# Decoder layer on one core: ten of sixteen states taken through both channel halves together, five scale operations, new tables of places

## What is computed

```python
def step(state, inp):
    d, b, c, u = inp
    dA = jnp.exp(d[..., None] * A)
    state = state * dA + (d * u)[..., None] * b[:, None, :]
    y = jnp.einsum('bdn,bn->bd', state, c)
    return (state, y)
```

```python
gamma_x = jnp.clip(jnp.max(jnp.abs(x), axis=-1, keepdims=True), 1e-05, None)
scale_x = 127.0 / gamma_x
x_dq = jnp.clip(jnp.round(x * scale_x), -128.0, 127.0) / scale_x
gamma_w = jnp.clip(jnp.mean(jnp.abs(w)), 1e-05, None)
w_dq = jnp.clip(jnp.round(w / gamma_w), -1.0, 1.0) * gamma_w
```

## Time and profile before

| | us |
|---|---|
| median of 3 runs | 993.59 |
| lowest and highest | 993.3, 995.66 |
| the profiled execution | 995.87 |
| span of its trace | 994.1 |
| PE busy | 818.1 |
| DVE busy | 797.5 |
| ACT busy | 591.6 |
| POOL busy | 479.0 |
| mean granted TensorE clock | 0.907 of full |

### The profile page before, as it was taken

How to read it: one execution, slowest core, us unless ns; L and a number is a source line. 1 busy time by engine, 2 the same in 40 slices (tenths; PEclk the granted TensorE clock), 3 DMA queues, 4 the chain that set the end, 5 groups by cost and what they waited for, 6 DMA issues and landing times.

```text
span 994.1 us, 11740 instructions
## 1 busy us (share of the span) xinstructions
PE 818.1 (82%) x4066; PEld 452.4 (46%) x4066; DVE 797.5 (80%) x953; ACT 591.6 (60%) x865; POOL 479.0 (48%) x283
## 2 busy tenths in 40 slices
PE   5778787465888889898877889896988799997798
PEld 1425445232553335564452434564564345663344
DVE  5869876696898988888897976978688997956874
ACT  3779779984277864633466766443366876443443
POOL 0546975684536625464437443365406664562010
PEclk9778997768799999998988999988999899999699
DMA  8677688767516636667436454575605675763000
GB/s 296 240 207 216 177 257 230 220 170 202 126 34 152 134 76 159 161 137 168 101 74 152 110 119 98 123 173 134 139 1 127 145 159 137 168 147 72 0 12 32
DMA packets 54815, 138.79 MB, mean 140 GB/s; under 512 B 7683, under 2 KB 8067, under 8 KB 54757
## 3 DMA queue, kind: packets, MB, share of 16 engines
q0 software_dynamic: 16128, 58.73, 31.1%
q1 hardware_dynamic: 38628, 79.32, 25.1%
HBM read 74.96 MB, written 4.35 MB: 80 GB/s over the span
## 4 chain that ended last, share of the span: by engine, by line
PE 42%; DVE 35%; ACT 14%; issue 7%; DMA 1%; DVEq 0%; POOL 0%; SPq 0%; ACTq 0%; POOLq 0%
PE bank L754 16%; DVE W L1738 11%; PE bank L967 7%; DVE PB L1727 6%; PE bank L783 4%; DVE U L1696 3%; PE bank L984 3%; ACT DEC L1203 3%; PE bank L802 3%; DVE BST L1673 2%; PE bank L861 2%; ACT W L1326 2%; PE bank L839 2%; DVE ARENA L1771 1%; DVE HAM L1891 1%
## 5 line engine op out<-in xcount | busy, mean ns | idle before, releaser
L1580 POOL TENSOR_TENSOR W<-W,CROW 128x1024 f32<-128x1024 f32 x128 | 321.1, 2509 | 239.2 <-DVE W L1738 188.1
L1738 DVE TENSOR_TENSOR_SCAN W<-DEC,PB 128x1024 f32<-128x1024 f32 x125 | 285.7, 2286 | 14.3 <-ACT DEC L1203 6.1
L1593 POOL DMA_DIRECT2D ACC<-W x112 | 98.4, 879 | 166.2 <-DMA ACC<-W 147.8
L1727 DVE TENSOR_TENSOR PB<-DU,PB 128x1024 f32<-128x1024 f32 x128 | 156.5, 1223 | 25.5 <-PE PB L923 21.2
L1203 ACT ACTIVATE DEC<-DT,ACOL 128x511 f32<-128x511 f32 x250 | 160.1, 710 | 21.4 <-DVE W L1738 20.3
L967 PE MATMUL bank<-W,ARENA 128*128 128x512 fp8e4 x512 | 127.8, 395 | 0.0
L923 PE MATMUL PB<-BC,ID 96*128 96x512 bf16 x128 | 50.7, 421 | 60.8 <-DVE W L1738 58.8
L1163 ACT ACTIVATE ARENA<-bank 128x512 f32<-128x512 f32 x56 | 32.3, 590 | 92.0 <-PE bank L754 51.0
L967 PEld LDWEIGHTS bank<-W,ARENA 128*128 128x128 bf16 x512 | 46.1, 100 | 66.2 <-issue 23.7
L1883 DVE SCALAR_TENSOR_TENSOR ARENA<-bank,SDQ,ARENA 128x512 f32<-128x512 f32 x64 | 46.8, 740 | 33.3 <-ACT ARENA L1303 15.3
L1303 ACT ACTIVATE ARENA<-bank,SDQ 128x512 f32<-128x512 f32 x64 | 43.1, 685 | 49.7 <-PE bank L967 49.4
(11 more groups left out here) (172 smaller groups left out, 1349.6 us busy)
## 6 DMA issues: line engine op xcount, KB each, us to landing
ACC<-W POOLq DMA_DIRECT2D x112, 512.0 KB, 4.8
CROW<-c_rows SPq DMA_DIRECT2D x128, 256.0 KB, 3.6
W<-in_wffn SPq DMA_DIRECT2D x27, 512.0 KB, 7.0
X<-in_wffn SPq DMA_DIRECT2D x21, 512.0 KB, 5.9
X<-in_x SPq DMA_DIRECT2D x7, 1024.0 KB, 8.2
out_dram<-X SPq DMA_DIRECT2D x16, 256.0 KB, 2.2
X<-in_ctxT SPq DMA_DIRECT2D x4, 512.0 KB, 4.7
ARENA<-in_x SPq DMA_DIRECT2D x1, 1024.0 KB, 6.4
```

The lines of the kernel that those rows point to most:

```text
L1580: pool.tensor_tensor(w, w, CROW[u % 2][:, :].unsqueeze(1).broadcast_to([P, 2, L]), ALU.mult)\
L1593: pool.dma_start(ACC[accumulator(u)][:, :, :], w, accum_op=ALU.add).then_inc(y_summed, 16)
L1727: dve.tensor_tensor(into, du, rows, ALU.mult).then_inc(dbu_done.sem, 1)
L1738: dve.tensor_tensor_scan(flat(W[u % 4]), flat(decay_of(u)), flat(PB[:, u % 2:u % 2 + 2, :]), 0.0, ALU.mult, ALU.add).then_inc(scan_done.se ...
```

## The change

**Order of the units.** In rows 2 to 4 states 0 to 5 of half 0 come first, then states 6 to 15 with half 0 and half 1 in turn, then states 0 to 5 of half 1. A unit with the same state as the one before it is `joined`: it has no spread and no row of C of its own. SPREAD_OF numbers the spreads, and their banks and the buffers CROW go by that number. The first unit of a pair keeps the spread's bank and writes the two others (`scan_bank`), so the next spread waits for that unit's scan (`spread_freed`).

**Step sizes of blocks 2 and 3.** On PE they move behind point r2, on ACT behind the gate's SiLU; in the list of products behind `wo`. DU for these blocks is made after unit 3. The skip term of half 1 moves from after r6 to after r5, ahead of the norm's `rstd`.

**Scales.** The division by 127 goes into the clipping, the reciprocal gives the scale directly, and the scales of both weights are made by one product each: five operations for eight.

**Tables.** All counts are set anew; the absolute sums, the ternary steps and the two reductions of row 1 have tables too (STEP_SUMS, STEP_TERNS, STEP_GAMMA), and a chunk's ternary step now stands one or two chunks behind its scaling.

```diff
+        out += on(four, [(b, "dt", 2), (b, "dt", 3)])
...
-        out += on(four, [(b, "dt", 2), (b, "dt", 3)])
...
-    [(('r', 0), 1), (('r', 1), 1), (('r', 2), 1), (('r', 3), 0), (('r', 4), 0), (('r', 5), 0), (('r', 6), 0),
-     (('r', 7), 2), (('r', 8), 4), (('f', 0, 0), 0), (('f', 0, 1), 0), (('f', 0, 2), 0), (('f', 0, 3), 2),
+    [(('r', 0), 2), (('r', 1), 1), (('r', 2), 1), (('r', 3), 0), (('r', 4), 1), (('r', 5), 1), (('r', 6), 0),
+     (('r', 7), 1), (('r', 8), 3), (('f', 0, 0), 0), (('f', 0, 1), 1), (('f', 0, 2), 1), (('f', 0, 3), 0),
...
-DU_AFTER = (28, 12)
+DU_AFTER = (28, 3)
...
+ALONE = 6
+HALVES_FIRST = [(h, n) for h in range(2) for n in range(N)]
+STATES_FIRST = ([(0, n) for n in range(ALONE)] + [(h, n) for n in range(ALONE, N) for h in range(2)]
+                + [(1, n) for n in range(ALONE)])
...
-    return b, j // N, j % N
+    return (b, *(STATES_FIRST if b else HALVES_FIRST)[j])
+def joined(u):
+    return u > 0 and unit(u)[::2] == unit(u - 1)[::2]
+def spread_freed(k):
+    return FIRST_WITH[k - 1] if FIRST_WITH[k - 1] < LAST_WITH[k - 1] else LAST_WITH[k - 2]
+def scan_bank(u):
+    upper = SPREAD_OF[u] % 2
+    return upper if u == LAST_WITH[SPREAD_OF[u]] else 1 - upper
...
@@ c_row (SP) @@
+                if joined(u):
+                    return
+                k = SPREAD_OF[u]
-                if u >= 2:
-                    sp.wait_ge(*hc_done.at(0, u - 1))
+                if k >= 2:
+                    sp.wait_ge(*hc_done.at(0, LAST_WITH[k - 2] + 1))
...
@@ spread_b, units (PE) @@
-                if u >= 2:
-                    pe.wait_ge(*scan_done.at(0, u - 1))
+                k = SPREAD_OF[u]
+                if k >= 2:
+                    pe.wait_ge(*scan_done.at(0, spread_freed(k) + 1))
...
-                    spread_b(u)
+                    if not joined(u):
+                        spread_b(u)
...
@@ step (PE) @@
                     units(b, "r", 2)
+                    step_size(b, 2)
+                    step_size(b, 3)
...
                 units(b, "r", 8)
-                if new:
-                    step_size(b, 2)
-                    step_size(b, 3)
...
@@ step (ACT) @@
                     gate_z(f, t)
+                if new:
+                    act.preload_act_table_set("softplus")
+                    step_size(b, 2)
+                    step_size(b, 3)
                 exp_and_log()
...
                 decays(b, "r", 5)
+                if new:
+                    skip_term(b, 1)
                 rstd(f, 2)
...
-                if new:
-                    skip_term(b, 1)
...
                     decays(b, "q")
-                    act.preload_act_table_set("softplus")
-                    step_size(b, 2)
-                    step_size(b, 3)
                     act.preload_act_table_set("silu_and_others")
...
@@ inputs_b, scan (DVE) @@
-                rows = PB[:, 2 * (u % 2), :].unsqueeze(1).broadcast_to([P, 2, L])
-                if u % 2:
+                rows = PB[:, 2 * (SPREAD_OF[u] % 2), :].unsqueeze(1).broadcast_to([P, 2, L])
+                if scan_bank(u):
...
@@ row_scales (DVE) @@
-                dve.tensor_scalar(AMC[:, :], AMX[:, :], 1e-5, None, ALU.max).then_inc(q_step.sem, 1)
+                dve.tensor_scalar(AMC[:, :], AMX[:, :], 1e-5, 1.0 / 127, ALU.max, ALU.mult).then_inc(q_step.sem, 1)
                 dve.wait_ge(*q_step.at(f, 2))
-                dve.reciprocal(RIN[:, :], AMC[:, :]).then_inc(q_step.sem, 1)
+                dve.reciprocal(SXQ[:, :], AMC[:, :]).then_inc(q_step.sem, 1)
+                dve.tensor_tensor(SDQ[:, :, :], AMC[:, :].unsqueeze(1).broadcast_to([P, 2, TT]),
+                                  GAM[:, 0:2].unsqueeze(2).broadcast_to([P, 2, TT]), ALU.mult).then_inc(q_step.sem, 1)
                 dve.wait_ge(*q_step.at(f, 3))
-                dve.tensor_scalar(SXQ[:, :], RIN[:, :], 127.0, None, ALU.mult).then_inc(q_step.sem, 1)
-                dve.wait_ge(*q_step.at(f, 4))
-                for i in range(2):
-                    dve.tensor_scalar(SDQ[:, i, :], AMC[:, :], GA127[:, i:i + 1], None, ALU.mult)\
-                       .then_inc(q_step.sem, 1)
-                    dve.tensor_scalar(RSC[:, :, i], SXQ[:, :], GAI[:, i:i + 1], None, ALU.mult)\
-                       .then_inc(q_step.sem, 1)
+                dve.tensor_tensor(RSC[:, :, :], SXQ[:, :].unsqueeze(2).broadcast_to([P, TT, 2]),
+                                  GAI[:, 0:2].unsqueeze(1).broadcast_to([P, TT, 2]), ALU.mult).then_inc(q_step.sem, 1)
```

More of the change, by code:

```diff
@@ L348, with spread_over @@
 BIAS_AFTER = 7
-DU_AFTER = (28, 12)
-def spread_over(steps, first):
+DU_AFTER = (28, 3)
+def spread_over(steps, first, total=TOTAL):
     at, n = [], first
@@ L357, in spread_over @@
         for point, count in places:
-            here[point] = [u for u in range(n, n + count) if u < TOTAL]
+            here[point] = [u for u in range(n, n + count) if u < total]
             n += count
         at.append(here)
-    assert n - first == TOTAL
+    assert n - first == total
     return at
@@ L367, with last_unit, rounded_in @@
 DECAY_AT = spread_over(STEP_DECAYS, 2)
+FIRST_LOADS = 14
+LOADS_AHEAD = 2
+SUM_AT = spread_over(STEP_SUMS, 0, 24)[0]
+TERN_AT = spread_over(STEP_TERNS, 0, 25)[0]
+GAMMA_AT = spread_over(STEP_GAMMA, 0, 2)[0]
+def last_unit(point):
+    here = [p for p, _ in STEP_UNITS[0]]
+    return max((u for p in here[:here.index(point) + 1] for u in UNIT_AT[0][p]), default=-1)
+def rounded_in(k):
+    return [m for m in range(24) if (m + 2 if m < 16 else m + 1) == k], [k] if k < 24 else []
 def units_at(b, point):
@@ L649, in load_abs, with before @@
                 sp.dma_start(ABS_STAGE[i % len(ABS_STAGE)], wffn[i]).then_inc(w_abs[i % len(ABS_STAGE)], 16)
+            def before(j):
+                return max((m for m in range(j) if tern_buffer(m) == tern_buffer(j)), default=None)
             def load_tern(j):
-                before = [m for m in range(j) if tern_buffer(m) == tern_buffer(j)]
-                if before:
-                    sp.wait_ge(tern_done, before[-1] + 1)
+                if before(j) is not None:
+                    sp.wait_ge(tern_done, before(j) + 1)
                 else:
@@ L707, in _ @@
                     sp.dma_start(BROW[64 * g + 3 * i:64 * g + 3 * i + 3, :], parts[:, g, :]).then_inc(brow_loaded, 16)
-            for j in range(UNITS):
+            loaded = 0
+            for j in range(-1, UNITS):
                 if j + 2 == UNITS:
                     store_c(1)
-                c_row(j + 2)
-                for i in abs_at(j):
-                    if i + len(ABS_STAGE) < WCH:
-                        load_abs(i + len(ABS_STAGE))
-                if j == 14:
-                    for m in range(4):
-                        load_tern(m)
-                for m in tern_at(j):
-                    if m + 4 < WCH:
-                        load_tern(m + 4)
+                if j >= 0:
+                    c_row(j + 2)
+                for point, sums in SUM_AT.items():
+                    for i in sums if last_unit(point) == j else ():
+                        if i + len(ABS_STAGE) < WCH:
+                            load_abs(i + len(ABS_STAGE))
+                if j == FIRST_LOADS:
+                    for loaded in range(4):
+                        load_tern(loaded)
+                for point, slots in TERN_AT.items():
+                    for k in slots if max(last_unit(point) - LOADS_AHEAD, FIRST_LOADS) == j else ():
+                        while loaded + 1 < WCH and set(rounded_in(k)[0]) & {before(loaded + 1)}:
+                            loaded += 1
+                            load_tern(loaded)
             residual_rows(0)
@@ L1185, in step_size @@
                 key = (b, "dt", e)
+                assert b == 0 or decayed[0] > max(u for u in range(TOTAL) if unit(u)[:2] == (b - 1, e // 2))
                 act.wait_ge(*R.full_at(*key))
@@ L1216, in decays @@
             def decays(b, *point):
-                if b == 0:
-                    for u in units_at(b, point):
-                        for m in tern_at(u - 1):
-                            ternary(m)
                 for u in decays_at(b, point):
@@ L1224, in decays @@
                 if b == 0:
[L1225 to L1228 removed]
+                    for i in SUM_AT[point]:
+                        abs_sums(i)
+                    for k in TERN_AT[point]:
+                        for m in rounded_in(k)[0]:
+                            ternary(m)
+                        for m in rounded_in(k)[1]:
                             ternary_scaled(m)
```

98 lines of the change are left out of this document (52 added, 46 removed), and 195 rows, old and new, of tables (STEP_DECAYS, STEP_GAMMA, STEP_SPREADS, STEP_SUMS).

## The result

| | before | after |
|---|---|---|
| median, us | 993.59 | 981.03 |
| lowest and highest | 993.3, 995.8 | 979.59, 981.95 |
| profiled execution | 995.87 | 981.07 |
| its span | 994.1 | 979.3 |
| mean granted TensorE clock | 0.907 | 0.902 |

The ratio is 0.9859, with a 95% interval of 0.9844 to 0.9874. That is 1.4% or 14.0 us of 994; the two medians lie 12.6 us apart. They differ because the five times of before fall into two groups, near 993.4 and 995.7, and the median takes the lower one. The forecast was 978, with a range of 963 to 995.

The account below looks back on a forecast made before the run. No engine was taken as full: the kernel is a relay between PE, DVE and ACT. Terms -7.6 - 9.0 - 0.5 = -17.1 took the median 993.59 to 976.5, stated as 978 us, range 963 to 995.

Parts of the forecast that it names:

- Part 1: 30 spreads go in rows 2 to 4, saving matmul time and PE and DVE waits: -7.6 us, ends 0 and -29.
- PE carries 42% of the chain, so 3.9 us of it is on the path: Matmul time of 24 removed spreads in feed-forward and attention, 9.4 us, counted by PE's chain share: 3.9 us.
- the 24 removed have 24/65 of the waits: Removed spreads' share of PE and DVE waits in feed-forward and attention: 7.4 us, half of it, 3.7, taken as gain.
- below 15 us: part 1 is right: Sign: PE's and DVE's waits around the spreads fall together below 15 us from 300 us on.
- Part 2: Step sizes of blocks 2 and 3 leave the feed-forward entry for behind the gate's SiLU: -9.0 us, ends -11.7 and +4.8.
- in return DVE's idle now holds a unit: Row 4: V's delay costs +3.2, but DVE's idle 4.08 us before 722.45 holds a unit of 3.5 us.
- Part 3: Scales in five operations, gaining only at tile 0 of the last row: -0.5 us, ends 0 and -3.5.
- Part 4: 30 C row loads go, but nobody waits for POOL there: 0, ends 0 and -5.
- Part 5: Tables: row 1's units, absolute sums and weight rounding placed anew with the same work: 0, ends -4.5 and +4.5.
- rival A: The change works as forecast: 968 to 987 us, chance 0.55.
- Rival B: PE's and DVE's slack takes the spread gain and one entry of two survives: 989.0 us, chance 0.12.
- Rival D: Slower: held banks stop PE before V and its clock may fall to 1.2 GHz: 1000 us, chance 0.14.

Follow-up runs that it names:

- copies: The changed kernel with each of the 30 shared spreads issued twice, one right behind the other, into the same bank: 980.69 us, 0.9865.
- unshared spreads at fitted places: The changed kernel with row 1 as before, no spread or C row shared, the spreads of rows 2 to 4 placed by its trace: 978.53 us, 0.9844.
- part 2 by itself, on the new counts: The kernel before with after's unit and decay counts for rows 2 to 4, fitted spreads, and the step sizes of blocks 2 and 3 moved: 988.03 us, 0.9932.
- new counts alone: The kernel before with after's unit and decay counts for rows 2 to 4 and spreads fitted to them, nothing else: 991.44 us, 0.9975.
- part 2 alone: The kernel before with only the step sizes of blocks 2 and 3 moved behind the gate's SiLU, all tables as before: 999.78 us, 1.0053.
- evened ternary slots: The changed kernel with the 25 ternary slots of row 1 one or two to a point, none of four: 977.51 us, 0.9832.
- the structure alone: The changed kernel with every table of places as before and no spread or C row shared: 995.57 us, 1.0018.

## Why the prediction was right in its number and wrong in its parts

From the kernel before to after, in the order in which the runs can be chained (difference of ratios times 994 us):

| step | us |
|---|---|
| new counts of rows 2 to 4, spreads fitted | -2.5 |
| step sizes moved (part 2), on these counts | -4.3 |
| five operations (-2.0 by itself), skip term, joined order, DU | -8.7 |
| sharing spreads and C rows | -2.6 |
| row 1's tables | +4.1 |
| sum | -14.0 |

**Part 1, -7.6: wrong.** The step "PE carries 42% of the chain, so 3.9 us of it is on the path" found no support: copies that take 6.9 us of PE cost 0.2 in the trace, where 42% would be 2.9. A share of the chain is an average, and these matmuls stand where PE has slack. That the removed spreads stood in slack too is argued from this, not shown. The step "the 24 removed have 24/65 of the waits" failed. The waits do fall, 58.8 to 31.1 us, but unshared spreads at fitted places wait 34.8 against 36.7. On the new counts they went with the places, not with the spreads, so the test that I named (below 15 us: part 1 is right) couldn't tell the one from the other. Measured: -2.6, within 0 to -5, and -5.2 by the traces.

**Part 2, -9.0: mechanism right, and incomplete.** From before to after the three entries changed by -0.5, -4.7 and -2.2 where I had -1.0, -3.9 and -4.1, and that with all the other edits in them; part 2 by itself, on the new counts, is -4.3. The 2.6 us between the square and the first gate came as costed: 4.49 us before, 1.91 after in row 3, and 5.70 and 3.13 in row 4. Row 4 fell short because the projection ran 2.6 us longer at a lower clock (last section). Against the new counts alone, part 2 with the edits that came with it takes 5.5 and 6.2 us off entries 3 and 4. V of row 4 in the kernel with part 2 alone starts 1.41 us after K for want of the bank, and the transposes come at 728.75, where I had worked out 728.2 for a projection that began 0.6 earlier. What I stated as "in return DVE's idle now holds a unit" was no side remark: without it the sign turns. The move costs 5.2 us on the old counts and gains 4.3 on the new ones. The condition belonged in the list of rivals with a price.

**Part 3, -0.5: a term mis-sized.** 2.0 (interval 1 to 3). I gave the last row 0.5 for tile 0 alone, but its scales are on the path for more than one group (0.6 and 0.85 us at the first two): 1.8 us from the last WO to the end.

**Part 4, 0: right.** **Part 5, 0: wrong on both sides.** In row 1 the end "one block later, +4.5" came true (+4.1), for the reason that I named (up to four steps together), and with it the sign of being wrong "ACT's rounding in row 1 holds PE". For rows 2 to 4 I counted only the units that left the entry, and gave the bodies nothing from the counts. The new counts alone give 2.9 + 6.4 us in bodies 3 and 4, against 7.8 lost in the entries and body 2. In body 4 DVE's idle went from 24.3 us before to 18.3 in after, with 110.8 and 110.9 us of work, and PE's from 13.5 to 10.6. Which unit's move did it was not followed up. Two readings of mine were off without changing a term: from 130 to 213 us ACT was busy for 78.8 of 83 us and not without a gap, and the first unit that needs DU of blocks 2 and 3 is unit 7.

That the sum came near is luck. Of the forecast -17.1, sharing gave 5.0 less than its term and row 1 cost 4.1 that I had at nothing. Parts 2 and 3 together with the new counts and the joined order gave 15.5 where I had 9.5. The errors cancelled to 3 us, and 981 was inside rival A's span. Rival B came nearest on part 1: slack takes at least the copies. Rival D was the real risk: part 2 on the old tables took 999.8 us, what D had for the whole change, though its V ran at full clock. In after it didn't come. The two held banks meet a DVE that has a unit to do, PE's wait before V is 0.98 us, and the clock at V stayed at full speed:

```profile
715.00:735.00 20.00, 17.23 (x92) 10.85 (x90) 18.15 (x32) 14.20 (x22) 9.13 (x6) 0.99 0.29 68
```

On the table load: in after the load of 487.82 is followed by Softplus at 489.11 and the next load at 490.40.

```profile
487.82 1.28 ACT L1541 ACT_TABLE_LOAD   x1
489.11 1.27 ACT L1274 ACTIVATE DT<-bank,DTB 128x512 f32<-128x512 f32 x2
490.40 1.28 ACT L1436 ACT_TABLE_LOAD   x1
491.69 0.60 ACT L1249 ACTIVATE ARENA<-bank 128x512 f32<-128x512 f32 x1
```

A switch costs 1.3 us here. The Trainium skill, "ScalarE: Activation LUTs", section "What ACT_TABLE_LOAD costs", has 2.66 with a drain of 1.38. These rows agree with the load itself, which it has at 1.283, and show no drain; the measurement decides.

**The fastest kernel** is after with row 1 as before: 976.4 us, 0.9818 (0.9798 to 0.9838). Its four times lie between 974.5 and 980.1. The evened ternary slots come to 0.9832, and their interval overlaps.

## What to carry to other kernels

When an order written by hand is retuned together with a change of structure, neither can be priced with the other left as it was. Here, without sharing, the structure alone was +1.8, the counts alone -2.5 and both together -15.5 us. Undoing an edit under tables tuned for it measures the misfit (48 us); with the places fitted to the trace first, the same edit cost about 3 us (0 to 5). Work taken from an engine counts only where the engine has no slack. Put a copy of it back and look, since neither its share of the chain nor the waits around it tell; and check in the trace how much time the copies really put back (6.9 us here, not 12.6).
